# Spreading the softmax inverses by fp32 products, with reciprocals and projections moved to other periods

## The reference

```python
qkv = jnp.einsum('bsm,qhdm->bqhsd', xn, W_qkv)          # 16 heads of 64
qk_rot = qk * cos + _rotate_half(qk) * sin              # the first 32 of 64 dims of Q and K
scores = jnp.einsum('bhqd,bhkd->bhqk', Q, K)
attn = jax.nn.softmax(jnp.where(causal, -jnp.inf, scores) / sqrt(DK), axis=-1)
out = jnp.einsum('bhqk,bhkd->bhqd', attn, V)            # then times W_o
gates = top 2 of softmax(xn @ router_w + router_b)
x + attention(xn) + sum_e gates[e] * gelu(xn @ w1[e]) @ w2[e] + gates[E] * xn
```

## Time and profile before

| | |
|---|---|
| median of three runs | 1490.87 us (1490.24 to 1496.87) |
| profiled execution: its own time, its span | 1500.74 us, 1499.0 us |
| mean granted TensorE clock | 0.965 |
| busy | PE 1254.0 us (84%), DVE 1195.7 (80%), ACT 1122.6 (75%), POOL 858.6 (57%) |

### The profile page before, as it was taken

The page is one execution under the profiler, slowest core; times in us unless marked ns, Lnnn a source line. Parts: engine busy times, 40 slices in busy tenths (PEclk is TensorE's granted clock), DMA queues, the critical chain, the costliest instruction groups (busy, mean ns, idle before and its releaser), DMA issues.

```text
span 1499.0 us, 46446 instructions
## 1 busy us (share of the span) xinstructions
PE 1254.0 (84%) x15156; PEld 940.5 (63%) x15157; DVE 1195.7 (80%) x4018; ACT 1122.6 (75%) x3606; POOL 858.6 (57%) x1194
## 2 busy tenths in 40 slices
PE   1416999888888898895999999888888889888888
PEld 1404666666666666664889898566666666666666
DVE  5788877777777887783777777889988889889886
ACT  6415888877787787784878887878777777777786
POOL 3254777777777777773000000767777777666775
PEclk9757999999999999997999999999999999999999
DMA  9621433333333333333232322333333333333330
GB/s 290 204 56 38 101 73 73 74 72 72 74 72 74 72 80 79 75 83 111 72 88 84 87 84 75 77 80 79 80 82 92 91 84 80 89 91 89 85 80 27
DMA packets 115831, 130.12 MB, mean 87 GB/s; under 512 B 11568, under 2 KB 75312, under 8 KB 115376
## 3 DMA queue, kind: packets, MB, share of 16 engines
q1 hardware_dynamic: 107056, 110.26, 30.6%
q0 software_dynamic: 8576, 17.33, 3.8%
HBM read 28.85 MB, written 31.59 MB: 40 GB/s over the span
## 4 chain that ended last, share of the span: by engine, by line
PE 28%; DVE 22%; DMA 17%; POOL 16%; issue 13%; ACT 4%; POOLq 0%; DVEq 0%; SPq 0%; ACTq 0%
DMA sorted_x_dram<-stage,slots 17%; PE bank L1102 6%; PE bank L1103 6%; PE bank L1104 6%; DVE arena L956 4%; POOL sorted_x_dram L497 3%; POOL arena L476 3%; PE bank L1173 3%; DVE arena L919 2%; DVE arena L918 2%; POOL arena L456 2%; PE bank L1184 2%; POOL arena L457 2%; ACT probs L643 2%; PE bank L1211 2%
## 5 line engine op out<-in xcount | busy, mean ns | idle before, releaser
L643 ACT ACTIVATE probs<-arena,neg_max 128x128 f32<-128x128 f32 (+1 forms) x1024 | 452.3, 446 | 110.5 <-DVE neg_max L956 108.5
L956 DVE CUSTOM_DVE_ANT_0 arena<-bank,causal 128x128 f32<-128x128 f32 (+1 forms) x1024 | 302.3, 349 | 46.6 <-PE bank L1173 46.1
L507 POOL DMA_INDIRECT stage<-sorted_y_dram,slots x128 | 130.5, 1020 | 257.9 <-DVE arena L919 238.6
L1184 PE MATMUL bank<-ident,probs 128*128 128x128 f32 x1536 | 212.6, 275 | 13.5 <-ACT probsT L626 10.7
L633 ACT ACTIVATE o_whole<-bank 128x256 f32<-128x256 f32 x256 | 97.7, 382 | 151.5 <-PE bank L1195 85.2
L497 POOL DMA_INDIRECT sorted_x_dram<-stage,slots x128 | 133.3, 1041 | 128.6 <-DMA sorted_x_dram<-stage,slots 104.2
L1184 PEld LDWEIGHTS bank<-ident,probs 128*128 128x128 f32 x1536 | 177.2, 142 | 39.6 <-issue 18.4
L643 ACT ACTIVATION_READ_ACCUMULATOR probs<-arena,neg_max 128x1 f32 x1024 | 194.7, 190 | 0.0
L1102 PE MATMUL bank<-arena 128*128 (+1 forms) x864 | 183.2, 238 | 1.5 <-DVE arena L1076 1.5
L476 POOL TENSOR_TENSOR arena<-o_whole,arena 128x256 f16<-128x256 f32 x256 | 172.0, 672 | 21.0
L1103 PE MATMUL bank<-arena 128*128 (+1 forms) x864 | 182.7, 238 | 0.0
(11 more groups left out here) (152 smaller groups left out, 3258.8 us busy)
## 6 DMA issues: line engine op xcount, KB each, us to landing
arena<-arena SPq DMA_DIRECT2D x256, 256.0 KB, 3.8
arena<-sorted_x_dram SPq DMA_DIRECT2D x72, 128.0 KB, 2.2
sorted_y_dram<-stage SPq DMA_DIRECT2D x72, 128.0 KB, 1.8
sorted_x_dram<-arena SPq DMA_DIRECT2D x3, 2304.0 KB, 17.8
arena<-experts_dram SPq DMA_DIRECT2D x8, 512.0 KB, 5.6
out_dram<-acc SPq DMA_DIRECT2D x32, 128.0 KB
sorted_x_dram<-arena SPq DMA_DIRECT2D x1, 2368.0 KB, 19.1
sorted_x_dram<-stage,slots POOLq DMA_INDIRECT x128, 2.5
```

Of the source, the lines that this page charges most:

```text
L643: last = nc.scalar.activation(probs[:, s % 4, at:at + w], masked[:, s % 4, at:at + w], ACT.Exp, bias=neg_max[:, s % 4, t:t + 1], scale=-1. ...
L956: last = nc.vector.tensor_tensor_reduce(out=masked[:, (s + i) % 4, at:at + w], in0=SC[i][:, at:at + w], in1=causal[:, at:at + w], scale=1. ...
L1184: last = nc.tensor.transpose(TP[s % 2][:, k * P:(k + 1) * P], probs[:, s % 4, k * P:(k + 1) * P], ident[:])
```

## The change

The inverses are spread by fp32 products of the inverse itself with the fp32 identity; the two fp16 parts, their semaphores, the fp16 identity and the factor of 64 go. The reciprocals are made for one pair in each period, on DVE right behind the next pair's masks. `turn_sums` comes one period earlier for a pair, behind the units and ahead of the transposes, and takes over the wait for `o_scaled`. `o_copy` waits for the products with V and no longer for the spread inverses. Sums have four places, not eight. In the usual samples the unit "rest" 0 of two samples ahead moves from period 5 to period 3, where it stands ahead of "v_high" 1; units of the sample two ahead come first in a period, and "rest" no longer comes last.

```diff
-AHEAD = ((5, "rest", 0), (6, "rope", 0), (7, "rest", 1))
+AHEAD = ((3, "rest", 0), (6, "rope", 0), (7, "rest", 1))
+AHEAD_OPENING = ((5, "rest", 0), (6, "rope", 0), (7, "rest", 1))
...
-QUAD = 4
-SUMS = 2 * QUAD
+SUMS = 4
...
-    steps = [(p, kind, j, b if kind == "v_high" else b - 1 if kind == "y" else b + 1)
-             for p, kind, j in (OPENERS if b in (0, MID) else USUAL) if nearer or kind in ("v_high", "y")]
-    steps += [(p, kind, j, b + 2) for p, kind, j in AHEAD if further]
+    opening = b in (0, MID)
+    steps = [(p, kind, j, b + 2) for p, kind, j in (AHEAD_OPENING if opening else AHEAD) if further]
+    steps += [(p, kind, j, b if kind == "v_high" else b - 1 if kind == "y" else b + 1)
+              for p, kind, j in (OPENERS if opening else USUAL) if nearer or kind in ("v_high", "y")]
     steps += [(p, kind, j, b + 1) for p, kind, j in VALUES if nearer]
-    return sorted(steps, key=lambda step: (step[0], step[1] == "rest" or step[0] == 6 and step[1] == "v_low"))
+    return sorted(steps, key=lambda step: step[0])
...
             def o_copy(J, j):
 
-                act.wait_ge(inv_turned, J + 1)
+                act.wait_ge(pv_done, 2 * J + 2)
...
-            def invert(N, n):
-
-                dve.wait_ge(exp_done, QUAD * N + QUAD)
-                of = slice(n % 2 * QUAD, n % 2 * QUAD + QUAD)
-                inv, hi, lo = inv_total[:, of, :], inv_parts[:, 0, of, :], inv_parts[:, 1, of, :]
-                nc.vector.reciprocal(inv, total[:, of, :]).then_inc(inv_done, 1)
...
-                nc.vector.tensor_scalar(hi, inv, W_SCALE, None, ALU.mult).then_inc(inv_hi, 1)
-                dve.wait_ge(inv_hi, N + 1)
-                nc.vector.scalar_tensor_tensor(lo, inv, W_SCALE, hi, ALU.mult, ALU.subtract).then_inc(inv_ready, 1)
+            def invert(J):
+
+                dve.wait_ge(exp_done, 2 * J + 2)
+                if J >= 2:
+                    dve.wait_ge(inv_turned, J - 1)
+                of = slice(J % 2 * 2, J % 2 * 2 + 2)
+                nc.vector.reciprocal(inv_total[:, of, :], total[:, of, :]).then_inc(inv_done, 1)
...
                     masks(b, 2 * p)
+                    then = past(b, p, 1)
+                    if then:
+                        invert(8 * then[0] + then[1])
                     for kind, j, of, u, psum in units_at(b, p):
                         if kind == "rope":
                             turn(j, u, psum, of)
...
+            def turn_sums(b, j, at):
+
+                pe.wait_ge(inv_done, 8 * b + j + 1)
...
+                for t in range(TPS):
+                    for i in range(2):
+                        of = inv_total[:, j % 2 * 2 + i, t:t + 1].broadcast_to([P, DK])
+                        last = mm(INV[j % 2][64 * i:64 * i + 64, t * P:(t + 1) * P], of, ident[:], start=True, stop=True)
+                last.then_inc(inv_turned, 1)
...
                     scores(b, 2 * p, parity, at == OPENING)
-                    then = past(b, p, INV_LAG)
-                    if then:
-                        turn_sums(*then)
                     for kind, j, of, u, psum in units_at(b, p):
                         unit(kind, j, of, of % 2, psum, bank_free(u))
+                    ended = past(b, p, PV_LAG)
+                    if ended:
+                        turn_sums(*ended, at)
                     then = past(b, p, T_LAG)
                     if then:
                         transposes(*then, then[0] == 0)
-                    then = past(b, p, PV_LAG)
-                    if then:
-                        attend(*then, at)
+                    if ended:
+                        attend(*ended)
```

More of the change, by code:

```diff
@@ L61 @@
 LO_HI = ((1, 0), (0, 1), (0, 0))
-T_LAG, PV_LAG, OUT_LAG, INV_LAG, SPLIT_LAG, BACK_LAG = 1, 2, 2, 3, 4, 2
+T_LAG, PV_LAG, OUT_LAG, COPY_LAG, SPLIT_LAG, BACK_LAG = 1, 2, 2, 3, 4, 2
 DVE_TURNED = (2, 4, 6, 8)
-QUAD = 4
-SUMS = 2 * QUAD
+SUMS = 4
 OPENING, FORMER, TURN, REOPEN, LATTER, FINAL = range(6)
@@ L173, in attention_and_experts @@
         inv_total = sb("inv_total", [P, SUMS, TPS], F32)
-        inv_parts = sb("inv_parts", [P, 2, SUMS, TPS], F16)
-        ident_h = sb("ident_h", [P, P], F16)
         o_whole = sb("o_whole", [P, 2, SEQ], F32)
@@ L220, in attention_and_experts @@
             "s_ready", "s_masked", "exp_done", "inv_done", "t_ready", "pv_done"))
-        inv_hi, inv_ready, inv_turned = (sem(n) for n in ("inv_hi", "inv_ready", "inv_turned"))
+        inv_turned = sem("inv_turned")
         t_out = [sem("t_out_dve"), sem("t_out_act")]
@@ L235, in attention_and_experts @@
         block = ctx.enter_context(nc.Block())
-        MADE = 7
+        MADE = 6
         ZEROED = 3 + E + 1 + 3
@@ L440, in _ @@
             nc.gpsimd.iota(grid_i, pattern=[[1, TILES]], base=0, channel_multiplier=0).then_inc(made, 1)
-            pool.wait_ge(made, MADE - 1)
-            nc.gpsimd.tensor_copy(ident_h[:], ident[:]).then_inc(made, 1)
             for i in range(NL):
@@ L639, in exps @@
                     act.wait_ge(t_ready, G - 3)
-                if not (at_first and s < SUMS) and s % QUAD == 0:
-                    act.wait_ge(inv_done, G // QUAD - 1)
+                if G >= SUMS and s % 2 == 0:
+                    act.wait_ge(inv_done, G // 2 - 1)
                 for t, (at, w) in enumerate(((0, P), (P, 2 * P))):
@@ L652, in sample @@
                     turned(past(b, p, OUT_LAG))
-                    then = past(b, p, INV_LAG)
+                    then = past(b, p, COPY_LAG)
                     if then:
@@ L982, in o_scale @@
                 dve.wait_ge(inv_turned, J + 1)
-                nc.vector.scalar_tensor_tensor(o_whole[:, j % 2, :], INV[j % 2], UNSCALE, o_whole[:, j % 2, :],
-                                               ALU.mult, ALU.mult).then_inc(o_scaled, 1)
+                nc.vector.tensor_tensor(o_whole[:, j % 2, :], INV[j % 2], o_whole[:, j % 2, :], ALU.mult).then_inc(o_scaled, 1)
             def y_add(b, t, u, psum, former):
@@ L1016, in sample @@
                             turn(j, u, psum, of)
-                    then = past(b, p, INV_LAG)
+                    then = past(b, p, COPY_LAG)
                     if then:
                         o_scale(8 * then[0] + then[1], then[1])
-                    then = past(b, p, 2)
-                    if then and p % 2 == 0:
-                        invert(4 * then[0] + then[1] // 2, then[1] // 2)
                     for kind, j, of, u, psum in due(b, p, 2):
@@ L1038, in rest_of @@
             def rest_of(b, at):
+                invert(8 * b + 7)
                 o_scale(8 * b + 5, 5)
-                invert(4 * b + 3, 3)
                 o_scale(8 * b + 6, 6)
@@ L1205, in attend @@
                     pe.wait_ge(o_scaled, 8 * b + j - 1)
+                for t in range(TPS):
[3 more added lines that the diff above has]
+                last.then_inc(inv_turned, 1)
+            def attend(b, j):
+                if j % 4 == 0:
+                    pe.wait_ge(v_ready, 4 * b + (2 if j == 0 else 4))
                 for i in range(2):
@@ L1224, in sample @@
                         transposes(*then, then[0] == 0)
-                    then = past(b, p, PV_LAG)
-                    if then:
-                        attend(*then, at)
+                    if ended:
+                        attend(*ended)
             def rest_of(b, at):
-                turn_sums(b, 5)
+                turn_sums(b, 6, at)
                 transposes(b, 7, False)
[L1232 to L1235, removed]
+                attend(b, 6)
+                turn_sums(b, 7, at)
+                attend(b, 7)
                 for kind, j, of, u, psum in units_at(b, PAIRS):
```

3 lines of the change are left out of this document (removed).

## The result

The changed kernel takes 1620.8 us (median of 4 runs, 1613.4 to 1627.6), the kernel before 1491.7 beside it: a ratio of 1.086, 95% interval 1.080 to 1.092. I had predicted 1520 with a range of 1475 to 1540: the direction was right, the size over four times too small (+29 forecast, +129 measured). The two profiled executions lie closer together than the medians, 112.7 us apart: the one before took 1500.7 us, more than any of the timed ones, the one after is the fastest of its four. What follows explains these 112.7 us; the other 16 are not accounted for.

The account below looks back on a forecast made before the run. POOL's sends bound former samples, DVE delaying TensorE latter ones; then the ring: 14 x 0.9 + 13 x 1.2 = 28.2 us, first and last samples making +32 on 1490.9, leaned 3 down: 1520, range 1475 to 1540 (own range 1498 to 1543).

Parts of the forecast that it names:

- The ring: Usual samples, first `stack_q` issue through "rest" 0, y and periods 5 to 7 to next issue: 36.3 us latter, 36.2 former.
- the waits foretold: ACT's `rest_high` waits for the DMAs, 2 to 3 us in each of 27 samples; the y waits for `rest_low`.
- the landing of the last: Last of four `stack_q` DMAs lands 6.7 us behind the first issue in latter samples, about 7 in former ones.
- TensorE's price: Spreading by fp32 products, +0.22 us, and one more change of tiling, 0.10: +0.32 us a period, +2.56 a sample.
- The added change of tiling: TensorE's array goes from 64 columns to full and back once more each period: 0.10 us, bounds 0 and 0.15.
- TensorE's sum: TensorE's work in a usual sample without waits: 30.6 us before, 33.2 us after the change.
- DVE's relief: L970 and L972 go, 0.96 us in period 0; without waits for L972, some 0.6 us left, latter samples 33.8 us.
- The new wait for `o_scaled`: `turn_sums` waits for `o_scaled` of two pairs before, satisfied in DVE's preceding period: costed at nothing.
- rival 1: DMAs land sooner or L481 comes earlier: latter samples 33.8 us, former ones stay with POOL; 1477 us, chance 0.15.
- Rival 2: Samples of 35.0 to 35.3 us, TensorE's waits turn from inverses to y: 1486 to 1497, say 1492 us; chance 0.20.
- Rival 3: Without L970 and L972 holding POOL, former samples gain 1.4 us each: about 1458 us, chance 0.05.
- Rival 4: fp32 products of the array's two halves don't run side by side, +0.44 us a period: 1580 us, chance 0.05.

Follow-up runs that it names:

- the best version: Changed kernel with "rest" 0 in period 5 and `turn_sums` right behind the scores, ahead of the units: 1465.9 us, ratio 0.974; again 1464.0, 0.972.

## Why the prediction was right or wrong

**The ring: right in kind.** "rest" 0 decides, as said: the waits foretold of `rest_high`, `rest_low` and the y are there in each of 27 samples, and moving that one unit back takes the loss away. POOL ceased to be the former samples' bound, as said.

**The step that failed is the size of the ring**, in three terms. First, "I take the landing of the last at 1093.3, 6.7 us behind the first issue": until `rest_high` starts it is 7.5 to 8.9, mean 7.8 in the latter samples and 8.2 in the former, against 6.7 and 7.0 (the landing itself some 0.2 earlier, at 7.3 in sample 23). I took the fall of the DMA share for the landing. At 27 samples that is 31 us, as much as the whole forecast. Second, the clock had no term at all. I carried the 1.00 of the earlier trace rows over, though by my own forecast TensorE stood 36.3 - 33.2 = 3.1 us in each sample. It stood 3.0 to 5.0 us, and where the clock fell, y to period 5 took 4.9 to 6.2 us and not 3.6. That is 38 us. Third, in former samples the first issue came at 12.9 and not 11.7: 17 us. I had given them 0.4 less than the latter ones because DVE has no combine in period 0. But `mix` (L904) took 2.70 us for its two operations, beside four of POOL's. These rows of the former samples show it (us busy, mean ns), of the kernel before:

```profile
L907 DVE TENSOR_SCALAR acc<-acc,small 128x128 f32<-128x128 f32 x28 | 11.0, 433 | 0.0
```

and of the changed one:

```profile
L904 DVE TENSOR_SCALAR acc<-acc,small 128x128 f32<-128x128 f32 x28 | 35.3, 1299 | 0.0
```

Part of this moved there from L970, whose 171 to 1174 ns I had counted as shed: in the kernel before L970 ran from 229.30 to 230.45, beside POOL's L481 (229.28 to 230.42), and both operations of `mix` behind it took 0.59. With L970 and L972 gone and the rest as before (fp32 products in place) `mix` takes 744 ns, so about 0.6 us a sample moved. The rest came with the ring: the same code takes 634 ns with "rest" 0 put back. In sample 3 TensorE waits 1.13 us for the `rest_low` behind `mix`. That the later issue follows from it is borne out by the run with "rest" 0 behind "v_high" 1, where both kinds of sample occur, as samples 2 and 5 show:

```profile
198.67 2.69 DVE L904 TENSOR_SCALAR acc<-acc,small 128x128 f32<-128x128 f32 x2
...
310.28 1.40 DVE L904 TENSOR_SCALAR acc<-acc,small 128x128 f32<-128x128 f32 x2
```

The first issue comes 12.9 us into the sample in each of the five whose `mix` took 2.7 us, and at 11.6 to 12.2 in eight whose `mix` took 0.6 to 1.7; only sample 14, the last of the stretch, has it at 15.05 with a short `mix`.

The ring's sum of 36.3 had no room for any of these: of the range given for it, 35.3 to 37.3, only the two quietest latter samples are at the upper end, and the other five whose clock didn't fall take 37.4 to 37.6. The range of the time was also added up wrongly: 1 us either way on 27 samples is 27 us about 1520, so 1493 to 1547 and not 1498 to 1543. The measured time is far outside of both.

**TensorE's price: right.** The spreading takes 0.59 us (0.56 forecast), +0.25 on 0.34. The added change of tiling was priced at 0.10 between bounds of 0 and 0.15; it takes 0.15: the transposes 0.80 us behind the spreads and 0.75 behind units (1294.63 to 1295.43; 1171.19 to 1171.94), and from the last unit to the spreads some 0.09. So TensorE's sum is 30.6 + 8 x 0.40 = 33.8 us and not 33.2. Without the added change it is 30.6 + 8 x 0.25 = 32.6; the best version's usual latter samples take 32.7.

**DVE's relief: right in the latter samples**, where a usual sample without the ring was forecast at 33.8 and takes 34.2. The forecast was near it partly by luck: its price for TensorE was 0.6 too low and the wait it left, 0.6, was some 0.2 too long. It brought nothing to the former ones, as rival 1 had it. The new wait for `o_scaled`, costed at nothing, cost nothing in the changed kernel; in the best version TensorE waits 20.5 us for it in the former samples, where POOL sets the pace.

**The rivals.** Rival 1 (no ring, 1477) is not what happened, but its time is what the kernel takes with "rest" 0 put back: 0.988 to 0.990 of 1490.9 is 1473 to 1476. Rival 2 (ring and savings cancel) fell with samples of 37.3 us and more. Rival 3 (POOL released by the loss of L970 and L972) fell in the fp32 products in place: both are gone and former samples take 35.7 and 36.0 us beside 36.0, not 1.4 less. Rival 4 (fp32 halves not side by side) fell with 0.59 us for eight instructions.

## What to carry to other kernels

A unit may move forward only as far as what it overwrites has been read: measure from the first issue of the reading DMAs to the instruction that waits for the last, not to the fall of the DMA share, and add it to the way round from there to the next issue. If that ring is longer than the bound engine's sum, every us of it is paid in each turn, and a TensorE that stands some us for it can pay again at half its clock. When an operation is removed that was long only because another engine held it, ask which operation will stand there next.

## What the runs showed that I had not expected

- TensorE's granted clock fell to 0.50 in 4.00 us of wait (sample 25) and stayed at 1.00 through 3.02 us (sample 23). Between these two, 1.0 us more from the first issue to `rest_high` became 3.3 us more of the sample (37.3 and 40.6). With waits of 3.1 to 3.3 us both happened.
- `mix`, two operations of 128x128 fp32, took 433 ns each in the former samples before and 1299 after. In sample 3 it spans POOL's L453 to L473 (242.73 to 245.4). The Trainium skill, "SBUF — State Buffer", section "SBUF: two separate sides", states that DVE and GpSimd lock each other out of a shared pair of ports for whole instructions; the trace agrees that DVE is held, though by the profile's starts DVE began 0.11 us ahead of POOL, and the rule would give the ports to whoever starts first.
- A change of the array's tiling inside a stream of matmuls cost 0.05 us (transposes behind spreads) and 0.09 us (spreads behind units), with no wait beside it. The step from fp16 units to fp32 transposes, both on the full array, has no such gap in the best version: the last unit starts at 1171.08, 0.11 us before the transposes, as units follow one another.
